# Second attention on one Trainium2 core: four splitting operations, ScalarE's copy of the shift, and its rows in two lots of three transfers

## The reference

```
qkv = x @ w_attn                       # x is layer-normed, q: 16 heads of 8, k, v: 8 each
att = einsum('bhqd,bkd->bhqk', q, k) * scale
att = where(causal, att, -inf); att = softmax(att)
y = einsum('bhqk,bkd->bhqd', att, v) ; out = y @ w_proj
```

## Time and profile before

| | before |
|---|---|
| median of 3 runs | 826.43 us (826.15 to 827.19) |
| the profiled execution's own time | 826.32 us |
| its span | 824.6 us |
| granted TensorE clock, mean over the span | 0.915 |

### The profile page before, as it was taken

One profiled execution on the slowest core, in us unless ns is written; L12 is line 12 of the kernel. 1 busy time (PEld: TensorE's weight loads), 2 busy tenths in 40 slices (PEclk: granted clock), 3 DMA queues, 4 the chain that ended last, 5 costly groups with the idle time before them and its releaser, 6 DMA issues. The chain is left out here.

```text
span 824.6 us, 14720 instructions
## 1 busy us (share of the span) xinstructions
PE 658.2 (80%) x4409; PEld 408.9 (50%) x4409; DVE 567.6 (69%) x1843; ACT 348.2 (42%) x748; POOL 348.9 (42%) x510
## 2 busy tenths in 40 slices
PE   1589898987008999999965779899898989898684
PEld 1346565655005788777842234445454535353353
DVE  8378888886862322444366978798979898884373
ACT  0422223311703222323321047677676767676751
POOL 0165555661027777677511014343434344333320
PEclk9999999999558999999965669999999999999995
DMA  9300000000411222222234304030303031200020
GB/s 295 97 1 1 0 1 0 0 2 1 144 38 49 43 42 36 39 42 40 24 76 62 45 11 59 4 60 10 53 14 51 21 43 26 37 2 4 1 77 27
DMA packets 40353, 32.47 MB, mean 39 GB/s; under 512 B 3608, under 2 KB 36936, under 8 KB 40280
## 3 DMA queue, kind: packets, MB, share of 16 engines
q1 hardware_dynamic: 30448, 23.51, 13.2%
q0 software_dynamic: 7840, 6.86, 5.7%
q10 hardware_dynamic: 1992, 1.21, 0.9%
HBM read 13.60 MB, written 8.13 MB: 26 GB/s over the span
## 5 line engine op out<-in xcount | busy, mean ns | idle before, releaser
L1613 ACT ACTIVATE pexp<-wide 128x512 f32<-128x512 f32 (+2 forms) x384 | 181.5, 535 | 108.8 <-PE wide L1802 107.3
L1544 POOL TENSOR_SCALAR_AFFINE_SELECT pexp<-pexp 128x256 f32<-128x256 f32 x256 | 105.0, 414 | 202.5 <-ACT pexp L1613 200.3
L1419 DVE CUSTOM_DVE_ANT_0 masked<-bank,mask_qk 128x384 f32<-128x384 f32 (+3 forms) x356 | 154.4, 480 | 22.0 <-PE bank L1753 21.1
L1802 PE MATMUL wide<-qT,kTe 128*128 128x256 bf16 (+3 forms) x512 | 121.8, 305 | 10.2 <-ACT pexp L1613 5.2
L1753 PE MATMUL bank<-kTm,qT 128*128 128x384 bf16 (+3 forms) x356 | 90.9, 323 | 16.4 <-DVE mx L1419 10.2
L1070 ACT ACTIVATE hT<-wide,b1T 128x512 f32<-128x512 f32 x64 | 44.0, 687 | 137.2 <-PE wide L1090 137.2
L1419 DVE CUSTOM_DVE_ANT_0 masked<-wide,mask_qk 128x256 f32<-128x256 f32 (+3 forms) x156 | 74.2, 498 | 18.6 <-PE wide L1753 18.6
L938 POOL DMA_INDIRECT x_row<-xln_dram,row_u x64 | 63.4, 991 | 52.8 <-DVE slot_tok L815 33.6
L1815 PE MATMUL bank<-pexp,vx 128*32 128x512 f32 (+3 forms) x1024 | 83.5, 444 | 0.0
L945 POOL DMA_INDIRECT x_dram<-yg,row_u x40 | 63.8, 1595 | 31.3 <-DVE yg L994 21.6
L561 POOL TENSOR_TENSOR kv<-kx,qv 128x1024 f32<-128x1024 f32 x32 | 62.3, 1949 | 24.1 <-PE wide L636 24.1
(11 more groups left out here) (232 smaller groups left out, 1086.7 us busy)
## 6 DMA issues: line engine op xcount, KB each, us to landing
qT<-qp SPq DMA_DIRECT2D x135, 64.0 KB
x_sb<-in_L_attn_x SPq DMA_DIRECT2D x8, 256.0 KB, 6.9
w_sb<-in_L_ffn_w SPq DMA_DIRECT2D x1, 2048.0 KB, 12.8
xln_dram<-rx SPq DMA_DIRECT2D x8, 256.0 KB, 2.3
out_x<-x_sb SPq DMA_DIRECT2D x8, 256.0 KB, 2.3
x_dram<-x_sb SPq DMA_DIRECT2D x5, 256.0 KB, 3.5
x_sb<-x_dram SPq DMA_DIRECT2D x5, 256.0 KB, 2.9
x_row<-xln_dram,row_u POOLq DMA_INDIRECT x64, 2.5
```

The lines of the kernel that those rows point to most:

```text
L1419: ins = nc.vector.tensor_tensor_reduce(out=masked[:, n % 4, at], in0=bank_of(n)[:, at], in1=mask_qk[:, T - w:T], scale=1.0, scalar=LEAST, ...
L1544: nc.gpsimd.affine_select(out=pexp[:, at, :, 0:P], in_=pexp[:, at, :, 0:P], pattern=[[0, 2], [1, P]], compare_op=ALU.is_ge, fill=0.0, base ...
L1613: nc.scalar.activation(pexp[:, exp_slot(b, 2 * step + h // 2), h % 2:h % 2 + nh, 0:w], psE[m % 3][:, 0:nh * w].rearrange("p (h t) -> p h t ...
L1802: ins = nc.tensor.matmul(psE[m % 3][:, hh * w:(hh + 1) * w], kTe[:, par, j * P:(j + 1) * P], qT[:, b % QB, 4 * qd + h + hh, j * P:T], star ...
```

## The change

The splits take four operations: the last subtraction writes the third part in bf16 itself. The transposes of the shift are issued at place A of step 13, behind the last unit of maxima of step 12 and the first scores of step 14. The copy to mT is done by ACT, at the beginning of step 13 ahead of the exponentials of step 14 (and before the first exponentials at the start). The shift's rows go in six DMAs, three for heads 0 to 3 (one for each part, 4 rows) and three for heads 4 to 15 (12 rows each), with a semaphore for each lot; the first scores wait for the first lot, the second quad's (step 4) for the second.

```
-        q_kvp, q_kv, q_kpart, q_qpart = Q("kv_psum"), Q("kv"), Q("k_parts", 5), Q("q_parts", 5)
+        q_kvp, q_kv, q_kpart, q_qpart = Q("kv_psum"), Q("kv"), Q("k_parts", SPLITS), Q("q_parts", SPLITS)   # SPLITS = 4
...
-        q_mTp, q_mT, q_mrow = Q("max_T_psum"), Q("max_T"), Q("shift_rows", 1, 16)
+        q_mTp, q_mT = Q("max_T_psum"), Q("max_T")
+        q_mrow = [Q(f"shift_rows_{lot}", PARTS, 16) for lot in ("first_quad", "other_quads")]
...
-        Q_SPLIT_STEPS = (4, 5)
+        Q_SPLIT = {(4, "A"): 1, (4, "C"): 2, (5, "A"): 3}
...
             for n in ops:
-                part = parts[n // 2]
                 if n:
                     engine.wait_ge(sig.sem, sig.at(b, n))
-                if n % 2 == 0:
-                    on.tensor_copy(part, whole if n == 0 else rest).then_inc(sig.sem, 1)
+                if n == SPLITS - 1:
+                    on.tensor_tensor(parts[-1], rest, parts[-2], ALU.subtract).then_inc(sig.sem, 1)
+                elif n % 2 == 0:
+                    on.tensor_copy(parts[n // 2], whole if n == 0 else rest).then_inc(sig.sem, 1)
                 else:
-                    on.tensor_tensor(rest, whole if n == 1 else rest, part, ALU.subtract).then_inc(sig.sem, 1)
+                    on.tensor_tensor(rest, whole if n == 1 else rest, parts[n // 2], ALU.subtract).then_inc(sig.sem, 1)
...
-        def dve_shift_T(dve, b):
-            dve.wait_ge(q_mTp.sem, q_mTp.at(b, 1))
-            dve.wait_ge(q_mrow.sem, q_mrow.at(b, 0))
-            nc.vector.tensor_copy(mT[:, :], psA[:, :].bitcast(BF16)[0:PARTS * HEADS, 0:T]).then_inc(q_mT.sem, 1)
...
+        def act_shift_T(act, b):
+            act.wait_ge(q_mTp.sem, q_mTp.at(b, 1))
+            for rows in q_mrow:
+                act.wait_ge(rows.sem, rows.at(b, 0))
+            nc.scalar.activation(mT[:, :], psA[:, :].bitcast(BF16)[0:PARTS * HEADS, 0:T], ACT.Copy).then_inc(q_mT.sem, 1)
...
             for s in range(STEPS):
+                if middle and s == SHIFT_STEP + 1:
+                    act_shift_T(act, b + 1)
...
             sp.wait_ge(q_mT.sem, q_mT.at(b, 1))
-            sp.dma_start(qT[QR:QR + PARTS, b % QB, :, :], mT[:, :]).then_inc(q_mrow.sem, 16)
+            for rows, lo, hi in ((q_mrow[0], 0, 4), (q_mrow[1], 4, HEADS)):
+                for n in range(PARTS):
+                    sp.dma_start(qT[QR + n:QR + n + 1, b % QB, lo:hi, :],
+                                 mT[n * HEADS + lo:n * HEADS + hi, :]).then_inc(rows.sem, 16)
...
             if step == 0:
-                pe.wait_ge(q_mrow.sem, q_mrow.at(b, 1))
+                pe.wait_ge(q_mrow[0].sem, q_mrow[0].at(b, PARTS))
                 pe.wait_ge(q_kTe.sem, q_kTe.at(b, 1))
+            if step == NT:
+                pe.wait_ge(q_mrow[1].sem, q_mrow[1].at(b, PARTS))
...
+                    if middle and (s, place) == (SHIFT_STEP + 1, "A"):
+                        pe_shift(pe, b + 1, front)
                     if place == "D":
                         if s % 2:
                             pe_values(pe, b, s - 1)
                             pe_values(pe, b, s)
-                        if middle and s == SHIFT_STEP:
-                            pe_shift(pe, b + 1, front)
```

More of the change, by code:

```diff
@@ L1190, in build @@
         Q = lambda name, per=1, step=1: signal("mqa_" + name, per, step)
+        SPLITS = 2 * PARTS - 2
         q_init = Q("buffers_set")
         q_xln, q_xTp, q_xT, q_qp = Q("xln", NT), Q("xT_psum"), Q("xT"), Q("q_psum")
-        q_kvp, q_kv, q_kpart, q_qpart = Q("kv_psum"), Q("kv"), Q("k_parts", 5), Q("q_parts", 5)
+        q_kvp, q_kv, q_kpart, q_qpart = Q("kv_psum"), Q("kv"), Q("k_parts", SPLITS), Q("q_parts", SPLITS)
         q_v, q_kx = Q("v"), Q("k_slots", PARTS)
@@ L1209, in build @@
         PER_QUAD = NM // NQ
-        q_smp, q_mx, q_mpart = Q("max_scores_psum", NM), Q("max", NM), Q("max_parts", 5)
-        q_mTp, q_mT, q_mrow = Q("max_T_psum"), Q("max_T"), Q("shift_rows", 1, 16)
+        q_smp, q_mx, q_mpart = Q("max_scores_psum", NM), Q("max", NM), Q("max_parts", SPLITS)
+        q_mTp, q_mT = Q("max_T_psum"), Q("max_T")
+        q_mrow = [Q(f"shift_rows_{lot}", PARTS, 16) for lot in ("first_quad", "other_quads")]
         NX = NQ * NT * 2
@@ L1362, in fill_k_slots, with split @@
             return ops(kx3[:, :, :, n, :], kp[:, n].unsqueeze(2).broadcast_to([P, NT, PARTS, L]))
-        def split(engine, on, sig, b, whole, rest, parts, ops=range(2 * PARTS - 1)):
+        def split(engine, on, sig, b, whole, rest, parts, ops=range(SPLITS)):
             for n in ops:
-                part = parts[n // 2]
                 if n:
                     engine.wait_ge(sig.sem, sig.at(b, n))
-                if n % 2 == 0:
-                    on.tensor_copy(part, whole if n == 0 else rest).then_inc(sig.sem, 1)
+                if n == SPLITS - 1:
+                    on.tensor_tensor(parts[-1], rest, parts[-2], ALU.subtract).then_inc(sig.sem, 1)
+                elif n % 2 == 0:
+                    on.tensor_copy(parts[n // 2], whole if n == 0 else rest).then_inc(sig.sem, 1)
                 else:
-                    on.tensor_tensor(rest, whole if n == 1 else rest, part, ALU.subtract).then_inc(sig.sem, 1)
+                    on.tensor_tensor(rest, whole if n == 1 else rest, parts[n // 2], ALU.subtract).then_inc(sig.sem, 1)
         def dve_q_parts(dve, b, ops):
@@ L1388, in pool_k_slots @@
         def pool_k_slots(pool, b):
-            pool.wait_ge(q_kpart.sem, q_kpart.at(b, 5))
+            pool.wait_ge(q_kpart.sem, q_kpart.at(b, SPLITS))
             pool.wait_ge(q_kTp.sem, q_kTp.at(b, 0))
@@ L1462, in dve_turn @@
                         dve_shift(dve, b + 1)
-                    if middle and s == SHIFT_STEP + 1 and place == "A":
-                        dve_shift_T(dve, b + 1)
                     if middle and s < SHIFT_STEP:
@@ L1472, in dve_turn @@
                         dve_stats(dve, b - 1)
-                    if front and s in Q_SPLIT_STEPS and place in "AC":
-                        dve_q_parts(dve, b + 2, (2 * Q_SPLIT_STEPS.index(s) + "AC".index(place) + 1,))
+                    if front and (s, place) in Q_SPLIT:
+                        dve_q_parts(dve, b + 2, (Q_SPLIT[s, place],))
         def dve_ln3_shift(dve, lo, hi):
@@ L1495, in mqa_dve @@
             dve_moe_stats(dve, 4)
-            dve_q_parts(dve, 0, range(1, 5))
+            dve_q_parts(dve, 0, range(1, SPLITS))
             nc.vector.memset(mask_qk[:, 0:T - P], 0.0)
@@ L1511, in mqa_dve @@
             dve_max(dve, 0, range(PER_QUAD, 2 * PER_QUAD), bank_at_start)
-            dve_q_parts(dve, 1, range(1, 5))
+            dve_q_parts(dve, 1, range(1, SPLITS))
             dve_max(dve, 0, range(2 * PER_QUAD, NM), bank_at_start)
             dve_shift(dve, 0)
-            dve_shift_T(dve, 0)
             dve_max(dve, 1, range(AHEAD), bank_in_turn)
@@ L1625, in act_yT, with act_turn @@
             nc.scalar.activation(y2T[:, :], psT[:, :], ACT.Copy).then_inc(q_yT.sem, 1)
-        def act_turn(act, b, tail=True, front=True):
+        def act_turn(act, b, tail=True, middle=True, front=True):
             for s in range(STEPS):
+                if middle and s == SHIFT_STEP + 1:
+                    act_shift_T(act, b + 1)
                 if s % NT == 0 and (s or b):
@@ L1676, in mqa_act @@
             act.wait_ge(s_shift.sem, s_shift.total(4))
+            act_shift_T(act, 0)
             act_exp(act, 0, 0)
             for b in range(B):
-                act_turn(act, b, tail=b > 0, front=b + 2 < B)
+                act_turn(act, b, tail=b > 0, middle=b + 1 < B, front=b + 2 < B)
             act_quad(act, B - 1, NQ - 1)
@@ L1690, in q_rows @@
             for n in range(PARTS):
-                queue.wait_ge(q_qpart.sem, q_qpart.at(b, 2 * n + 1))
+                queue.wait_ge(q_qpart.sem, q_qpart.at(b, min(2 * n + 1, SPLITS)))
                 for j in range(PARTS):
@@ L1779, in pe_shift @@
         def pe_shift(pe, b, front):
-            pe.wait_ge(q_mpart.sem, q_mpart.at(b, 5))
+            pe.wait_ge(q_mpart.sem, q_mpart.at(b, SPLITS))
             if front:
```

## The result

The changed kernel takes 814.71 us (median of 5 runs, 812.47 to 816.04); the kernel before took 826.70 in the five runs beside it (826.15 to 828.28). The ratio is 0.9853 with a 95% interval of 0.9831 to 0.9875: 12 us faster. Each ratio is to the kernel before in runs made beside it, and where a kernel has runs over 1.5% longer at a lower clock, the ratio leaves them out.

The account below looks back on a forecast made before the run. PE's queue was taken to set the 39.3 us turn, through three waits in steps 12 to 15. Gains of 6 x 1.17 + 0.34 + 0.27 + 0.24 = 7.9 us from 826.32 gave 818.4 us, range 814.8 to 825.6.

Parts of the forecast that it names:

- Four operations: Shift's split on DVE: the fifth operation is dropped, so the transposes start 0.25 us after the fourth starts.
- ScalarE's copy: Step 13: ACT's copy to mT takes 0.583 us; PE's bank-0 unit starts 1.15 us earlier, with the earlier transposes.
- Transposes behind the units of step 12: PE, steps 12 to 13: two pieces, some 0.2 to 0.34 us each, run before the transposes instead of after.
- Six transfers: SP, before the next sequence's first scores: three issues of 0.45 us and a 2.22 us tail, 3.63 us for 3.66.
- The cap: PE at the next sequence's first scores: it would arrive at 559.97 for 561.53, at most 1.56 us gained a turn.
- The start and the last hand-over: Outside the six turns: 0.27 us at the start, 0.24 at the first shift, 0.34 at the last hand-over.
- B: Rival at the transfers: issues of 0.76 us each, tail 2.22; 1.4 us gained, 825.0 us; chance 0.12.
- C: Rival at the transfers: issues of 0.76 us, tail 2.90, the transfer is late; 3.4 us lost, 829.7; chance 0.12.
- D: Rival inside the turn: PE's gain is lost waiting for another engine; 821.6 us if DVE, 824.2 if ACT; chance 0.18.

Follow-up runs that it names:

- e5: The changed kernel with five operations for the maxima again (q's and k's stay at four): 814.16 us, ratio 0.9870 to the kernel before.
- e6: The changed kernel with the copy to mT on DVE again, at step 13 place A: 825.02 us, ratio 0.9983 to the kernel before.
- e7: The changed kernel with the transposes at place D of step 12 again: 813.74 us, ratio 0.9876 to the kernel before.
- e1: The changed kernel with the shift's rows in the one transfer of before: 817.33 us, ratio 0.9896 to the kernel before.
- e4: The kernel before with only the six DMAs and two semaphores of the change added: 823.97 us, ratio 0.9991 to the kernel before.

## Why the prediction was wrong

The mechanism was right where it counts, and a size was off: the transfers. A second size, the cap on a turn's gain, was off with it.

- *Four operations*: 0.25 us a turn forecast, 0.23 measured (e5). The transposes start 0.28 us after the last operation does, where 0.25 was written.
- *ScalarE's copy*: 0.90 us of the 1.15 were its share; e6 measures 0.91. The bank-0 unit starts 1.09 us after the transposes, as worked out, the copy takes 0.59 us and the exponential behind it starts 0.94 us after the transposes, before 0.98.
- *Transposes behind the units of step 12*: they run early, as written, but e7 shows that this is worth nothing beside ScalarE's copy.
- *Six transfers*: the step that failed. Forecast 3.63 us from first issue to first scores, 0.03 less than before. Measured 3.04 at the last hand-over and 3.10 in the turns. Issues were dearer than taken (0.62 for 0.45), but the tail was 1.18 us where I took 2.22, and thereby under its own lower bound of 1.94. That bound came from a 256 KB store to HBM, which says nothing of a few rows between two places of SBUF. The 3.47 us that the prediction worked out by the Trainium skill's rule, outside its sum, were nearer but too long as well. PE no longer waits, and the turn wins 0.57 us where I gave it 0.03: 0.54 us in six turns is 3.2 of the 4.1 us by which the span's gain of 12.0 exceeds the forecast (the time around the span took 0.4 back).
- *The cap* of 1.56 us was also too low. I took what PE would win from the idle times in the rows (0.41 us for the transfer). These start from the modelled end of the piece before, and pieces overlap when they follow each other closely: start to start, the piece before the scores is followed after 0.22 us if nothing is late and was after 0.79. The wait was worth 0.57, as e1 and e4 both show, and the turn could win 1.7. The range's fast end (815.3 us, widened to 814.8) rests on this cap in all six turns: the transfer's own lower bound of 2.84 us would have let them win more, and the measured 3.04 to 3.10 lie inside its bounds. So the likeliest value missed by the transfer's size, and the range by the cap. With 3.10 us in the turns and 3.04 at the end, my sum gives 815.5 us under the cap and 814.7 without it. That this hits 814.71 is in part luck, since the smaller terms below were off both ways.
- *The start and the last hand-over*: 0.39 us until the first transposes (0.51 forecast), 0.96 until the second (0.76, with the dropped operation). The first full turn won 1.48 us, its transfer still being 0.2 late. The last won 1.97, more than the others because the dropped operation took 0.43 us there; the scores behind it won 0.42 more. Together the last hand-over won 0.89 us where 0.34 were forecast; the difference is again the transfer's (3.04 us for 3.63). The 0.31 us left behind the last scores have no part of the change in them: PE's clock stood at 0.50 at other times in the two profiles.
- *Rivals*: B's issues of 0.76 us (0.62 measured at the last hand-over, 0.64 in the turns) and C's tail of 2.90 were not there; D was not either, since all of a removed wait stayed removed.

## What to carry to other kernels

Read a wait on TensorE at the weight load too, since a product's record can be missing, and size it from start to start against the same two pieces where nothing is late; the idle time shown understated it by 0.16 us of 0.57 here. A transfer of 12 rows of 1 KB into three partitions was released 2.2 us after its issue started, one of 48 rows into three partitions after 3.6, so cut off what the next step needs first and send that as one transfer of its own. When two engines wait for each other at a hand-over, put independent work of the waiting engine right behind the instruction that feeds the chain: by the turns this was worth as much here as the transfers were (0.61 and 0.57 us).

## What the runs showed of the hardware

- One transfer of 48 rows of 1 KB into three partitions: 3.64 to 3.76 us from issue to release; 12 rows into three: 2.15 to 2.23; three transfers of 4 rows: 3.04 to 3.10 (3.30 in the first turn); three of 16 rows: 3.40 to 4.49, unevenly.
- PE's clock fell to 0.50 behind waits of 0.8 to 1.3 us in some turns of e4 and e6 and stayed there for 3 to 4 us, at a cost of 1.5 to 1.6 us each; in e6 it was every second turn, behind the same wait as in the others.
- Among runs of one kernel on one chip the time follows the mean granted clock: 821.98 us at 0.924, 830.29 at 0.906.
